# A graph layer with experts on one core: key-value stage in six iterations instead of seven, padding groups last, ScalarE alone normalising the opening's rows

## What is computed

```python
dst = (6250 * uniform ** 2.0)                    # sorted: low nodes have most edges
xn  = layernorm(x)
msg_sum = segment_sum(xn[src], dst); mean = msg_sum / max(count, 1)
gnn = relu(relu(mean @ W_l.T + b_l + xn @ W_r.T) @ W_ln.T + xn)
kv  = einsum(layernorm_per_head(k), layernorm_per_head(v)) / 6250   # over all nodes
mix = gelu((q @ kv + xn) @ w1 + b1) @ w2 + b2 + xn
x   = x + gnn + mix
x   = x + shared_ffn(layernorm(x)) + top-2 of 8 experts(layernorm(x))
```

## Time and profile before

| | us |
|---|---|
| median of 3 runs (lowest, highest) | 2538.97 (2537.24, 2541.27) |
| the profiled execution's own time | 2541.11 |
| its span, first to last instruction | 2539.1 |
| busy in the span: PE, PEld, DVE, ACT, POOL | 2140.6, 1655.5, 1105.4, 769.8, 1774.2 |
| mean granted TensorE clock | 0.924 of full speed |

### The profile page before, as it was taken

One profiled execution on the slowest core, in us unless ns is written; L12 is line 12 of the kernel. 1 busy time (PEld: TensorE's weight loads), 2 busy tenths in 40 slices (PEclk: granted clock), 3 DMA queues, 4 the chain that ended last, 5 costly groups with the idle time before them and its releaser, 6 DMA issues.

```text
span 2539.1 us, 61133 instructions
## 1 busy us (share of the span) xinstructions
PE 2140.6 (84%) x13164; PEld 1655.5 (65%) x13165; DVE 1105.4 (44%) x4278; ACT 769.8 (30%) x1954; POOL 1774.2 (70%) x1786
## 2 busy tenths in 40 slices
PE   0888666777999999999999999999999866488979
PEld 0444445555777777777777777787777643377768
DVE  8555434444454445444444444444444322222321
ACT  4344222222233323323332333233333201022323
POOL 1477577777777777777777777777777777757720
PEclk9899778888999999999999999999999976599989
DMA  8333344445656665666566566656665654878834
GB/s 266 96 105 106 101 116 118 118 118 151 189 166 174 185 183 162 181 183 184 153 189 183 165 176 182 188 158 182 185 185 152 180 145 107 263 239 263 262 104 135
DMA packets 273733, 424.97 MB, mean 167 GB/s; under 512 B 76425, under 2 KB 202185, under 8 KB 272938
## 3 DMA queue, kind: packets, MB, share of 16 engines
q0 software_dynamic: 94880, 231.75, 33.6%
q1 hardware_dynamic: 172058, 183.19, 22.2%
q10 hardware_dynamic: 6384, 6.42, 0.7%
HBM read 380.74 MB, written 40.48 MB: 166 GB/s over the span
## 4 chain that ended last, share of the span: by engine, by line
PE 45%; issue 18%; POOL 13%; DVE 8%; DMA 7%; DVEq 4%; ACT 2%; SPq 1%; POOLq 1%; ACTq 0%
POOL region L709 10%; PE p_agg L1734 7%; PE p_y L1971 6%; DMA region<-xn_d,idx_s 6%; PE p_h L1960 4%; PE p_h L1927 4%; PE p_y L1933 4%; PE p_agg L1771 3%; PE p_h L2058 3%; PE p_a L2089 2%; PE p_t L1774 2%; PE p_a L1917 2%; POOL out_rows L737 2%; PE p_h L2123 1%; DVEq L171 1%
## 5 line engine op out<-in xcount | busy, mean ns | idle before, releaser
L709 POOL DMA_INDIRECT region<-xn_d,idx_s x1566 | 1497.3, 956 | 582.0 <-issue 447.6
L1734 PE MATMUL p_agg<-region,winhot 128*32 128x258 f32 x3168 | 318.0, 424 | 113.1 <-DMA region<-xn_d,idx_s 86.0
L1158 DVE TENSOR_TENSOR late<-late,p_agg 128x258 f32 x218 | 92.1, 423 | 514.9 <-issue 299.0
L1971 PE MATMUL p_y<-region 128*128 128x256 f32 x1280 | 293.5, 382 | 0.0
L1734 PEld LDWEIGHTS p_agg<-region,winhot 128*32 128x32 f32 x3168 | 120.3, 116 | 264.2 <-issue 197.9
L1771 PE MATMUL p_agg<-part_s,placehot 96*128 96x258 f32 x528 | 183.5, 431 | 119.7 <-DVE part_s L1223 95.7
L1971 PEld LDWEIGHTS p_y<-region 128*128 128x128 f32 x1280 | 240.1, 190 | 47.4 <-issue 16.6
L888 ACT ACTIVATE work<-p_h,b1s_s 128x128 f32<-128x128 f32 x384 | 109.7, 368 | 494.8 <-PE p_h L1927 494.8
L1960 PE MATMUL p_h<-wkv_s,region 128*128 128x256 f32 x960 | 229.2, 389 | 2.3 <-issue 2.2
L1960 PEld LDWEIGHTS p_h<-wkv_s,region 128*128 128x128 f32 x960 | 177.5, 191 | 40.8 <-issue 19.7
L1933 PE MATMUL p_y<-w2s_s,work 128*128 128x256 f32 x768 | 203.9, 390 | 0.0
(11 more groups left out here) (302 smaller groups left out, 3202.8 us busy)
## 6 DMA issues: line engine op xcount, KB each, us to landing
region<-in_w1p SPq DMA_DIRECT2D x60, 1024.0 KB, 7.3
region<-in_w2p SPq DMA_DIRECT2D x60, 1024.0 KB, 7.0
region<-xn_d,idx_s POOLq DMA_INDIRECT x1566
rows_s<-slot_d SPq DMA_DIRECT2D x40, 258.0 KB
region<-in_x SPq DMA_DIRECT2D x7, 896.0 KB, 12.7
xn_d<-region ACTq DMA_DIRECT2D x7, 896.0 KB, 4.1
rows<-in_x SPq DMA_DIRECT2D x49, 128.0 KB
xnr_s<-xn_d SPq DMA_DIRECT2D x49, 128.0 KB
```

Source lines behind the costliest of these rows:

```text
L709: pool.indirect_dma_start(out=ring[b][:, u, 0:D], out_offset=None, in_=xn_d, in_offset=IND(ap=idx_s[:, b, u:u + 1], axis=0)).then_inc(s_ro ...
L1734: m = mm(p_win[j * WIN:(j + 1) * WIN, :], winhot[:, b % 2, PARTS[j][r], :], ring[b][:, PARTS[j][r], :], start=r == 0, stop=r == len(PARTS[ ...
L1971: m = mm(p_y[:, h, :], hid2_s[:, j, h * P:(h + 1) * P], w2p_s[0][:, j, :], start=j == 0 and h == 0, stop=j == KF - 1, skip_group_check=True)
```

## The change

`KI` is 6, and the 49 tiles are dealt over 24 slots by `kv_tiles`: two per slot and three in the last. The node stage begins with iteration 6. The three padding groups become the last three of iteration 65: the lists of indices, the copy of `dst` and the rows of lists that `next_rows` fetches are shifted by three groups. The first four groups are gathered at once, without waits, when the stores of `xn_d` have landed; for the padding groups POOL issues one plain transfer each. Their windows are set so that they match no row, and their tile to 0. In the opening ACT normalises all seven tiles of a chunk.

```diff
-KT = 7
-KI = -(-NT // KT)
+KI = 6
...
-BY_ACT = 4
...
         def rounds(it, b):
-            return it if b < PADG else it + 1
+            return it + 1
+        def kv_tiles(it, b):
+            slot = RING * it + b
+            return range(slot * NT // (KI * RING), (slot + 1) * NT // (KI * RING))
...
-            for b in range(PADG):
-                nc.gpsimd.memset(ring[b][:, :, 0:D], 0.0)
...
-            pool.reg_mov(group, 2 + PADG)
+            pool.reg_mov(group, 2)
...
-            def gather_edges(b):
-                pool.wait_ge(S["const"], 3)
-                pool.wait_ge(S["idx"], group)
-                pool.wait_ge(S["pass_"], group)
+            def gather_edges(b, free=False):
+                if not free:
+                    pool.wait_ge(S["const"], 3)
+                    pool.wait_ge(S["idx"], group)
+                    pool.wait_ge(S["pass_"], group)
...
+            def fill_padding(b):
+                pool.wait_ge(S["const"], 3)
+                pool.wait_ge(S["idx"], group)
+                pool.wait_ge(S["pass_"], group)
+                pool.dma_start(ring[b][:, 0, 0:D], xn_d[0:P, :]).then_inc(s_row[b], 16 * U)
+                pool.reg_add(group, group, 1)
-            for b in range(PADG, RING):
-                gather_edges(b)
+            for b in range(RING):
+                gather_edges(b, free=True)
...
-            with pool.Fori(KI, NI) as it:
+            with pool.Fori(KI, NI - 1) as it:
                 plan.look(word.now() >> RING)
                 word.look_up(it + 1)
-                step(True)
+                step(RING)
                 plan.after()
+            plan.look(word.now() >> RING)
+            step(RING - PADG)
+            plan.after()
...
-                for j in range(BY_ACT):
+                for j in range(XCH):
...
-                act.wait_ge(S["xn"], c + 1)
...
+                if c:
+                    dve.wait_ge(S["xna"], c)
                 own.step(V.reciprocal(rs_s[:, 0:XCH], sd_s[:, 0:XCH]))
...
-                for j in range(BY_ACT, XCH):
-                    xj = x_s[:, c * XCH + j, :]
-                    i = V.tensor_scalar(xj, xj, mv_s[:, j, 0:1], rs_s[:, j:j + 1], ALU.subtract, ALU.mult)
-                i.then_inc(S["xn"], 1)
...
-            V.tensor_scalar(span_s[0:1, :], tile_i[0:1, :], 7, None, ALU.arith_shift_right).then_inc(S["span"], 1)
+            own.step(V.tensor_scalar(span_s[0:1, :], tile_i[0:1, :], 7, None, ALU.arith_shift_right))
+            for i in range(2):
+                last = V.memset(span_s[0:1, i * NS:i * NS + 2 + PADG], 0)
+            last.then_inc(S["span"], 1)
...
+            own.step(V.memset(rel_s[:, 0:(2 + PADG) * U], 255.0))
...
-                    for j in SLOT[b]:
-                        m = KT * it + j
+                    for m in kv_tiles(it, b):
```

More of the change, by code:

```diff
@@ L23 @@
 RING = 4
-KT = 7
-KI = -(-NT // KT)
+KI = 6
 NKV = NT
-SLOT = ((0, 1), (2, 3), (4, 5), (6,))
-assert KI * KT == NT
 NI = -(-EDGES // (P * U * RING))
@@ L468, in first_lists @@
                 for b in range(RING):
-                    sp.dma_start(idx_s[:, b, :], idx[RING * NI - 1 - b:RING * NI - b, :, :].squeeze(0)
-                                 ).then_inc(S["idxin"], 16)
+                    row = RING * NI - 1 - PADG - b
+                    sp.dma_start(idx_s[:, b, :], idx[row:row + 1, :, :].squeeze(0)).then_inc(S["idxin"], 16)
             def shelf_lists():
@@ L748, in add_single, with step @@
                 pool.reg_add(added, added, 16)
-            def step(gather):
+            def step(groups):
                 for b in range(RING):
-                    if gather:
+                    if b < groups:
                         gather_edges(b)
+                    elif groups:
+                        fill_padding(b)
                     if b == 1:
@@ L780, in _ @@
             plan = Plan(pool, first=FIRSTS, second=SECONDS, add=ADDING, spread=SPREADING)
-            with pool.Fori(KI, NI) as it:
+            with pool.Fori(KI, NI - 1) as it:
                 plan.look(word.now() >> RING)
                 word.look_up(it + 1)
-                step(True)
+                step(RING)
                 plan.after()
+            plan.look(word.now() >> RING)
+            step(RING - PADG)
+            plan.after()
             with plan.rest():
                 with plan.left():
-                    step(False)
+                    step(0)
                     plan.advance()
@@ L1043, in pads_first @@
                 def pads_first(to):
-                    V.tensor_copy(to[:, 0:2 * U], dst32_s[:, NG * U:])
-                    return V.tensor_copy(to[:, 2 * U:], dst32_s[:, 0:NG * U])
+                    V.tensor_copy(to[:, 0:(2 + PADG) * U], dst32_s[:, (NG - PADG) * U:])
+                    return V.tensor_copy(to[:, (2 + PADG) * U:], dst32_s[:, 0:(NG - PADG) * U])
                 own.step(pads_first(dst_s))
@@ L1215, in enter_edges @@
                 keep_part(edges, 0)
-                dve.wait_ge(S["lists"], edges[0] * 16 + 16 * (len(SPANS) + 2 - SHELF))
+                dve.wait_ge(S["lists"], edges[0] * 16 + 16 * (len(SPANS) + 3 - SHELF))
                 next_rows(edges[0] + 1, 0)
@@ L1225, in next_rows @@
             def next_rows(it, b):
+                ahead, b_list = divmod(b + PADG, RING)
                 if isinstance(it, int):
-                    at = shelf_of(it) * RING
+                    at = shelf_of(it + ahead) * RING
                 else:
-                    at = dve.snap(shelf_of(it) * RING).with_bounds(min_val=0, max_val=(SHELF - 1) * RING)
-                V.tensor_copy(idx_s[:, b, :], lists_s[:, ds(at + (RING - 1 - b), 1), :].squeeze(1)).then_inc(S["idx"], 1)
+                    at = dve.snap(shelf_of(it + ahead) * RING).with_bounds(min_val=0, max_val=(SHELF - 1) * RING)
+                V.tensor_copy(idx_s[:, b, :], lists_s[:, ds(at + (RING - 1 - b_list), 1), :].squeeze(1)).then_inc(S["idx"], 1)
             def finish(edges, b):
@@ L1299, in kv_iteration @@
                 edges = begin(it)
+                if it + 2 >= SHELF:
+                    dve.wait_ge(S["lists"], 16 * (len(SPANS) + it + 3 - SHELF))
                 state(edges, 1)
@@ L1308, in kv_iteration @@
                         squares(m)
-                        if j == SLOT[b][0] and (it, b) != (KI - 1, RING - 1):
+                        if m == kv_tiles(it, b)[0] and (it, b) != (KI - 1, RING - 1):
                             finish(edges, b)
```

## The result

| | us |
|---|---|
| median before, 4 runs beside those of after (lowest, highest) | 2540.12 (2537.24, 2545.53) |
| median after, 4 runs (lowest, highest) | 2576.64 (2572.75, 2579.39) |
| ratio after to before | 1.014, 95% interval 1.0118 to 1.0162 |
| the profiled execution after: its own time, its span | 2575.58, 2573.6 |

The change costs 36.5 us on the medians and 34.5 us between the two profiled executions, where 20.4 us were forecast. The direction and two of the terms are right; some 15 us stand where the prediction had nothing, and so the time lies above the end of its range, 2567 us.

What follows compares the result with a forecast made beforehand. The prediction took POOL's transfers to bound the node stage and a serial chain the key-value stage. Terms: -9.9 us through the key-value stage, +30.3 for the blank iteration, +20.4 on 2538.97, so 2559.4 us; range 2546 to 2567.

Steps and rivals of the forecast that it cites:

- Opening: Opening, up to tile 0's sum of squares: 1.3 us gained, tile 0 at 89.8 us.
- The 0.7 us for gathers beside DVE's list chain: Opening: early gathers slow DVE's 24 copies, casts and tensor_scalars by 0.03 us each, 0.7 us.
- The 8.7 us: Rival, opening: each of DVE's 24 instructions might wait for a gather, 8.7 us, total 2567 us; chance 0.06.
- Key-value stage: Key-value stage: serial chain over tiles bounds; tile 48 at 277.2 instead of 287.1 us, 9.9 us earlier, opening included.
- That gathers end the stage: Rival, key-value stage: gathers rather than the chain end it at 262 us, 15 us less, total 2544 us; chance 0.06.
- The blank iteration: Node stage, iteration 52: no step runs, yet POOL pays four groups' gathers in full, 30.3 us.
- both rivals: Node stage: no blank at iteration 52, 2529 us, chance 0.06; blank cheap if PE bounds, 2537 us, chance 0.05.
- the first rival: Node stage: step 46 runs in iteration 52, the 30.3 us fall to the last iteration, total 2529 us; chance 0.06.
- So the node stage is as long as POOL's list of transfers: Node stage: POOL issues without a pause and bounds it; 1.26 us per gather, 30.3 us per four groups.
- End: Iteration 65: three padding groups become plain transfers while POOL is ahead; put at nothing, 0 to 3 us of gain.

Runs made afterwards that it cites:

- the loop moved: Changed kernel plus 162 one-element memsets at the start of DVE's program, which shift its node loop: 2561.63 us, ratio 1.0069 to 1.0102.
- ScalarE's rows alone: Kernel before with ACT normalising all seven rows of a chunk, nothing else changed: 2536.50 us, ratio 0.9981 to 1.0002.
- the two kernels that have it there: Changed kernel with iteration 52's count of finished tiles raised by one: 2565.75 us; changed kernel with all padding edges at the low end: 2566.47 us.
- the best version: Changed kernel plus a seventh group iteration without tiles, worked off in the key-value stage's closing steps: 2535.68 us, ratio 0.9975 to 0.9993.

## Why the prediction was wrong where it was

**Opening.** Right in kind, half in size: tile 0 came 2.6 us earlier instead of 1.3. The 0.7 us for gathers beside DVE's list chain were too much if anything: the chain took 23.3 us (from 44.31 to 67.62) against 22.7 before, the new memsets among it, and with ScalarE's rows alone, without those gathers and memsets, tile 0 came no earlier (88.6 us). The 8.7 us that a rule of the Trainium skill would have asked ("SBUF — State Buffer", section "Who interferes with whom") weren't paid; that rival is gone.

**Key-value stage.** Right: 277.8 for a forecast of 277.2 us, and 9.95 us at the node stage's first gather. It is so close by some luck: from tile 0 to tile 48 the chain took 189.3 us instead of 187.4, and the opening's extra 1.3 us made up for most of that. That gathers end the stage is gone too.

**The blank iteration.** Right in its place (iteration 52), its cause and its price: 30.56 for 30.3 us. In the changed kernel it isn't cheap, and it exists; both rivals fall. But the first rival's number was wrong as well: it called an iteration at the end "padding and beside other work", and the two kernels that have it there lose 21 us.

**"So the node stage is as long as POOL's list of transfers."** This step failed. It held for the kernel before, and the prediction carried it over as if nothing else were near. From iteration 9 to 15 PE and DVE needed 32.5 us for what POOL did in 33.0 (561.5 - 366.5 and 552.0 - 354.2 for six): the margin was half a microsecond an iteration. A turn of DVE's loop that was longer by about as much (idle 6.5 instead of 5.6 us) made PE and DVE the bound; over the nine steps before the pairs PE's lag behind the gathers grew to 9.7 us, and over the first pairs to 15, where gathers wait for passes (from 553 to 800 us POOL waits 6.7 us for PE's sums, before 1.5). The term that was missing is 14.8 us, and no rival of the prediction had it. Most of it is the time between two iterations on DVE for which "issue" is all that its own rows say: with the loop moved the stretch is 11.4 us shorter (1615.9 instead of 1627.3). Where the other 3.4 us come from isn't shown. With it the sum is -9.9 + 30.6 + 14.8 - 1.0 = 34.5 us, the difference of the two spans, as it must be, since the four stretches fill the span. With the loop moved the changed kernel comes to 2561.6 us, 23.4 above the kernel before, where the forecast had 20.4.

**End.** Put at 0 to -3; measured -1.0 us.

## What to carry to other kernels

Before a wait or an iteration is priced by one engine's list, compare that list with the next chain, stretch by stretch; a lead of half a microsecond in thirty isn't a bound to build on. Idle time that a profile gives to "issue" once in every turn of a loop is worth looking at: it can change with code far ahead of the loop, and then a change is blamed for a place in memory; the instruction transfers in that gap and a few idle instructions at the start show it. And work that has to fill an empty iteration is better put into a stretch in which all engines wait already.

## What the runs showed that was not expected

The turn of DVE's loop took 3.13 to 3.26 us in the kernels whose loop begins at 234 to 249 in a block of 256 instructions, and 3.57 to 3.75 us at 76 to 86 (medians, eleven kernels). What goes with it in the traces is the second instruction packet within the turn; what sets that packet's moment isn't shown. On this kernel the place is worth 11 to 15 us, where the best version gained 2.5.

PE loses twice by the wait at the turn, since it goes on at half the clock. In the changed kernel's iteration 11 it waits 6.27 us for DVE's copy; PE's rows, then the windows of those sums and of the next group's:

```profile
471.72 1.23 PE L1787 MATMUL p_agg<-part_s,placehot 96*128 96x258 f32 x2 [6.27 <-DVE part_s L1237]
472.88 1.94 PE L1750 MATMUL p_agg<-region,winhot 128*32 128x258 f32 x12
...
478.89 1.07 PE L1750 MATMUL p_agg<-region,winhot 128*32 128x258 f32 x12
```

```profile
471.80:474.60 2.80, 2.80 (x14) 0.99 (x14) 1.60 (x10) 0.00 (x0) 2.19 (x3) 0.50 0.39 113
478.90:479.90 1.00, 1.00 (x14) 0.40 (x13) 0.18 (x2) 0.36 (x2) 0.92 (x1) 1.00 0.42 127
```

The granted clock is 0.50 (1.2 GHz) and the twelve sums take 1.94 us; behind a run of products it is 1.00 (2.4 GHz), and they take 1.07. The longer wait adds nothing to that here: at the same place before, behind 5.02 us, the sums took as long.

```profile
476.20 1.23 PE L1771 MATMUL p_agg<-part_s,placehot 96*128 96x258 f32 x2 [5.02 <-DVE part_s L1223]
477.35 1.94 PE L1734 MATMUL p_agg<-region,winhot 128*32 128x258 f32 x12
```
